# Edge stage of a graph attention kernel: eight block numbers with one register load on TensorE and on VectorE

## The reference

```
qi = q[dst]
kj = k[src]
vj = v[src]
alpha = jnp.sum(qi * kj, axis=-1) / jnp.sqrt(jnp.float32(D))
m = jax.ops.segment_max(alpha, dst, num_segments=n)
ex = jnp.exp(alpha - m[dst])
denom = jax.ops.segment_sum(ex, dst, num_segments=n)
a = ex / (denom[dst] + 1e-16)
out = jax.ops.segment_sum(a[..., None] * vj, dst, num_segments=n)
```

## Time and profile before

| what | value |
|---|---|
| median of three runs | 1348.41 us |
| span of the profiled execution, first to last instruction | 1474.8 us |
| edge stage in it, first to last `prod` | 95.1 to 815.0 us |
| busy in the span: PE, DVE, POOL, ACT | 84%, 72%, 63%, 54% |
| DVE busy from 200 to 750 us | 426.0 of 550 us |
| TensorE clock granted from 200 to 750 us | 0.89 |
| block numbers loaded by PE, by DVE | 232, 261 |

### The profile page before, as it was taken

How to read it: one execution, slowest core, us unless ns; L and a number is a source line. 1 busy time by engine, 2 the same in 40 slices (tenths; PEclk the granted TensorE clock), 3 DMA queues, 4 the chain that set the end, 5 groups by cost and what they waited for, 6 DMA issues and landing times. The chain is left out here.

```text
span 1474.8 us, 24100 instructions
## 1 busy us (share of the span) xinstructions
PE 1233.3 (84%) x6835; PEld 952.7 (65%) x6835; DVE 1068.6 (72%) x2557; ACT 802.2 (54%) x2505; POOL 924.8 (63%) x885
## 2 busy tenths in 40 slices
PE   7988676766776777767676889999999999999998
PEld 3444454544444544545454478889798899999998
DVE  7646887777877777877788779886757655556655
ACT  1265857575847575666657555555543344444443
POOL 3366566666666665666664556866766477667765
PEclk9999989899888898888989999999999999999999
DMA  7477766676766666767675120101000000000002
GB/s 229 157 225 211 235 192 193 183 203 184 200 187 196 188 200 179 202 185 204 181 199 145 38 70 29 52 28 42 8 15 22 1 22 15 10 21 15 1 12 77
DMA packets 74087, 175.39 MB, mean 119 GB/s; under 512 B 11516, under 2 KB 36667, under 8 KB 73961
## 3 DMA queue, kind: packets, MB, share of 16 engines
q0 software_dynamic: 37632, 124.28, 30.3%
q1 hardware_dynamic: 34657, 48.25, 9.9%
q10 hardware_dynamic: 1672, 1.33, 0.3%
HBM read 159.91 MB, written 13.91 MB: 118 GB/s over the span
## 5 line engine op out<-in xcount | busy, mean ns | idle before, releaser
L694 POOL DMA_INDIRECT ring<-kv_rows,k_srcI x464 | 465.1, 1002 | 280.8 <-issue 121.5
L764 ACT ACTIVATE ring<-ring 128x64 f32<-128x64 f32 x1800 | 439.8, 337 | 15.0 <-issue 13.4
L1297 POOL TENSOR_TENSOR wm<-k_gf,wm 128x512 fp32r<-128x512 f32 (+2 forms) x224 | 259.6, 1163 | 143.4 <-DVE wm L1798 143.4
L1396 ACT ACTIVATE k_gf<-psF,k_scT 128x512 f32<-128x512 f32 (+2 forms) x224 | 162.3, 725 | 251.9 <-PE psF L1567 237.6
L814 PE MATMUL psA<-ring,oh 128*128 128x260 f32 x912 | 273.4, 428 | 6.6 <-DVE k_acc L1023 5.4
L784 PE MATMUL psQ<-k_q,ohT 128*128 x1392 | 221.1, 300 | 66.7 <-issue 63.3
L1798 DVE CAST wm<-k_gf 128x512 fp32r<-128x512 f32 (+2 forms) x224 | 160.2, 722 | 155.3 <-ACT k_gf L1396 155.3
L989 DVE TENSOR_TENSOR prod<-psQ,ring 128x512 f32<-128x512 f32 x232 | 157.5, 679 | 82.2 <-remote 28.3
L784 PEld LDWEIGHTS psQ<-k_q,ohT 128*128 128x128 bf16 x1392 | 128.8, 103 | 123.0 <-issue 93.9
L814 PEld LDWEIGHTS psA<-ring,oh 128*128 128x128 f32 x912 | 177.3, 216 | 33.8 <-ACT ring L764 6.3
L1029 DVE TENSOR_REDUCE alpha<-prod 128x8 f32<-128x512 f32 x232 | 155.7, 671 | 0.2
(11 more groups left out here) (283 smaller groups left out, 2644.9 us busy)
## 6 DMA issues: line engine op xcount, KB each, us to landing
ohT<-step_destinations SPq DMA_DIRECT2D x29, 512.0 KB
ring<-kv_rows,k_srcI POOLq DMA_INDIRECT x464
kv_rows<-kvst SPq DMA_DIRECT2D x25, 260.0 KB, 2.6
we<-in_L_ffn_W SPq DMA_DIRECT2D x16, 256.0 KB, 2.8
residual<-qst SPq DMA_DIRECT2D x25, 128.0 KB
xs<-in_x SPq DMA_DIRECT2D x2, 1024.0 KB, 9.1
resin<-residual SPq DMA_DIRECT2D x4, 512.0 KB, 4.5
we<-in_L_ffn_Wo SPq DMA_DIRECT2D x8, 256.0 KB, 2.8
```

Of the source, the lines that this page charges most:

```text
L694: nc.gpsimd.indirect_dma_start(out=ring[:, LT * (j % CP) + k, j // CP:j // CP + 2, :].rearrange("p t e -> p (t e)"), out_offset=None, in_= ...
L764: last = nc.scalar.activation(row[:, 0:D], row[:, 0:D], ACT.Copy, scale=row[:, D:HW_])
L1297: nc.gpsimd.tensor_tensor(low[:, i % 2, m, 0:w], gf[:, n % 4, 0:w], high[:, i % 2, m, 0:w], ALU.subtract).then_inc(s_gl, 1)
L1396: nc.scalar.activation(gf[:, n % 4, 0:cols(g)], ps, ACT.Relu, bias=bias, scale=scale).then_inc(s_ev, 1)
```

## The change

Both engines load eight block numbers at once, into eight registers, with one TENSOR_LOAD a chunk, and without the check of the bounds. PE does so in `expand` where `jj` is 0. DVE does so where it rescales; the registers then serve the rescaling and the eight additions that follow, and the load at the head of every `at` is gone. The values, the matmuls and the vector operations stay as they are.

```
+        def blocks(engine, first):
+
+            n = min(CP, STEPS - first)
+            _, got = nc.values_load_multi_w_load_instructions(
+                brow[0:1, first:first + n], engines=[engine], min_val=0, max_val=NB - 1,
+                skip_runtime_bounds_check_because="a step's block is a count of block borders, made on the chip between 0 and NB - 1")
+            return got
+
...
+            held = {}
+
             def expand(i, j, fresh):
...
-                blk = nc.tensor.value_load(brow[0:1, bass.ds(step, 1)], min_val=0, max_val=NB - 1)
+                if jj == 0:
+                    held[0] = blocks(mybir.EngineType.PE, step)
+                blk = held[0][jj]
...
                 if live(i, j, fresh, ADD_LAG):
                     b = step - ADD_LAG
-                    blk = nc.vector.value_load(brow[0:1, bass.ds(b, 1)], min_val=0, max_val=NB - 1)
+                    blk = held[0][b % CP]
...
-                    blk = nc.vector.value_load(brow[0:1, bass.ds(br, 1)], min_val=0, max_val=NB - 1)
+                    held[0] = blocks(mybir.EngineType.DVE, br)
+                    blk = held[0][0]
                     dve.wait_ge(s_mv, NV * m + V_FAC)
```

## The result

| | before | changed |
|---|---|---|
| median | 1349.61 us (17 runs, 1346.42 to 1351.88) | 1354.01 us (17 runs, 1346.56 to 1362.29) |
| span of the profiled execution | 1474.8 us (the one of the earlier trace rows) | 1344.9 us |

The ratio is 1.0036, with a 95% interval from 1.0022 to 1.0049: slower by 4.4 us where 7.3 us were forecast. Measured again later (experiment 10), the same kernel had 1.0006, from 0.9993 to 1.0018. The two intervals don't overlap: a small loss the first time, none the second. The medians give no gain in either.

What follows compares the result with a forecast made beforehand. The prediction took DVE's chain of vector instructions to bound the edge stage. Its terms, -3.5 + 14.8 - 4 = +7.3 us on the median of 1348.4 us, gave 1355.7 us, range 1336 to 1384 us.

Steps and rivals of the forecast that it cites:

- What bounds the kernel: Edge stage: DVE's chain of vector instructions bounds it in the runs, about 2.5 us a step, with PE ahead.
- The surplus of the profiled span: Edge stage: the profiled span's 126 us over the median run is idle time mostly not in the runs.
- Removed, 1: DVE's load and check in 232 steps, covered by queued vector work: 0 in seven steps of eight.
- Removed, 2: DVE's second load, in the step after the rescaling, goes: 0.12 us exposed a chunk, -3.5 us.
- Changed, 3: DVE's load of eight before the rescaling: 1.38 us with 0.87 us free, delaying the rescaling each chunk, +14.8 us.
- L: The length of one load of eight numbers, taken as 1.38 us, bounded between 0.31 and 2.46 us.
- the first rival: DVE's wide load is cheap, up to 0.87 us, so the rescaling isn't delayed: -7.5 us, 1341 us, chance 33%.
- the rival with 17%: The load of eight: 0.2 us for each further number, slower than before; chance 17%.
- Removed, 4: PE's load and check go in 203 steps, counting only where DVE waits for PE: -4 us.
- Changed, 5: PE's load of eight delays a chunk's first group by 0.9 us, covered by 1.5 us: 0.
- Nothing changes: The queue's deeper cover in the runs hides both the exposed 0.12 us and the rescaling's delay: 1348 us, chance 12%.
- my own sign of being wrong in substance: If L is small and nothing is gained, the runs have no exposed sequencer time at all.

Runs made afterwards that it cites:

- experiment 10: The changed kernel unaltered, measured again beside the kernel before: 1349.56 us, ratio 1.0006.
- 6: The kernel before, but from the 33rd step on SyncE copies the second tile of a step instead of its being gathered: 1333.23 us.
- 7: The changed kernel, but from the 33rd step on SyncE copies the second tile of a step instead of its being gathered: 1323.38 us.
- c0: The kernel before, unchanged, profiled a second time: 1349.05 us (one run), span 1347.4 us.
- experiment 1: The kernel before with PE's half of the change alone; VectorE keeps one load and check a step: 1347.98 us, ratio 0.9991.
- 2: The kernel before with VectorE's half of the change alone; PE keeps its load and check a step: 1352.69 us, ratio 1.0024.
- 3: The kernel before with one load a step kept on both engines, only the bounds check removed: 1351.19 us, ratio 1.0017.
- 12: The changed kernel with the comparison that makes `ohT` cut from 2048 columns to one from the fifth chunk on: 1338.89 us, ratio 0.9937 against experiment 10.

## Why the prediction was right or wrong

The sign and the range were right by luck, the reason was not. The forecast's +14.8 us is a cost that doesn't exist and its -7.5 us a gain that can't show; with the right length of the load the same reasoning would have said 1341 us.

- *What bounds the kernel.* Wrong. I said that VectorE's chain bounds the edge stage in the runs. It does in 6 and 7. In the kernels themselves VectorE first waits over 0.3 us for a gather at 335 us in c0 and at 271 us in the changed kernel; until then the gathers are ahead, though they run at their own pace from 148 us on. From there POOL's gathers hold the pace, 20.0 us a chunk and more. The step that failed is the first: I read 353 of 550 us of POOL as slack. Its busy time leaves out the 0.30 us between two gathers, and the profile's row for it had 121.5 us of "issue". 8 x 2 x 1.25 = 20.0 beside 19.5 us was there to be worked out.
- *The surplus of the profiled span.* That it isn't in the runs was right. That it comes with the profiler was no sound thought: c0 is profiled and has none, and 18 plain runs had it. Of the 39 waits ahead of the product that I laid to PE's results, lays 14 to PE.
- *Removed, 1.* 0 for seven steps, right: intervals of 2.18, 2.15, 2.61, 2.25 us and so on are the same in both.
- *Removed, 2*, -3.5 us: the pause did go, 2.47 to 2.34 us; its worth to the kernel was 0, since the gathers hold the pace. With half of the gathers it paid.
- *Changed, 3*, +14.8 us: mis-sized. L is 0.598 us, not 1.38; the spare time is 1.05, not 0.87. The term is 0. The mechanism exists, with L = 1.60 us, and even then cost 2.5 us and not 16. The measured L agrees with the first rival, "a wide load is cheap"; its time, 1341 us, failed by the same wrong bound. The 0.153 us that I took for each further number was an estimate, half a lone load. The 0.2 us a further number of the rival with 17%, which stands in the chances, no run shows: a further number took 0.042 us with 8 and (1.602 - 0.306) / 23 = 0.056 us with 24. That the load starts when the queue takes no more holds as far as this: in c0 26 of the 29 loads at L1040 start within 0.004 us of the start of the mask L1007, three vector instructions ahead of the rescaling. That a lone load's 0.306 us is a wait for an answer and not work, no run shows.
- *Removed, 4*, -4 us: 0, by experiment 1.
- *Changed, 5*: 0, right.
- *The rivals and the signs.* "Nothing changes", 1348 us, came nearest in time, but not for its reason: the exposed 0.12 us was there and went. L is small and nothing was gained, which was my own sign of being wrong in substance; what I would have concluded from it, that no sequencer time is exposed, is wrong too. PE's "issue" waits fell to a fifth, not an eighth, and a third of all its waiting there was left.
- *What is left.* The sum of true terms is 0, the measured difference 4.4 us once and 0.6 us once. Experiments 2 (+0.24%) and 3 (+0.17%) point to VectorE's half, with the reserve on the tail given there, and 10, the whole change, has no loss. A gather that begins while VectorE runs a mask or the comparison is longer, by 0.20 and 0.46 us on average, and the removed pause moves every such instruction by 0.12 us against POOL; that this is the cause was argued, not shown. Each of the two measurements has its median outside the other's interval, so something that differs between them matters as much as the change. It may be the chip; neither kernel was run twice on one known chip to tell.

No version here beats both kernels with the right output where the kernel before takes 1349 us. The largest handle that the runs show is not in the changed lines: the gathers' pace (6 and 7) and the comparison that lengthens them (12).

## What to carry to other kernels

Work out the period of every engine that issues work, from start to start and not from its busy time, before naming the bound: in c0 POOL was busy 306.8 of 400 us (77%) and held the pace. Time taken from an engine that then waits for another came back here as that wait (27.1 us on average with the pause, 33.1 without), and the row "who waited for it" shows it; but compare several profiles, since this row alone differed by 4 us between two kernels with the same code on VectorE. Profile the kernel before a second time when its span and its runs disagree.

## What the runs showed of the hardware

- A load of registers from SBUF took 0.306 us for one number, 0.598 for 8, 1.602 for 24: 0.04 to 0.06 us for each further one.
- An indirect gather of 128 rows took 0.946 us, and the next one started 0.305 us after its end, never later than 0.32 us while nothing held it; those pauses don't count as busy (307 gathers in 400 us of c0: 306.8 us busy). It took some 1.48 us (median) when it met the bf16 comparison of 2048 columns (by the five profiles of c0, 1 to 3 and the change, 124 gathers during which it was the last vector instruction running 0.1 us after their start took 0.46 us more on average). Without most of the comparison (12) the gathers of the stage's second half took 5.5 us in all beyond 0.946 us each, with it (10) 16.1. Why the comparison lengthens a gather, no run shows.
- The same holds for the masks (two SBUF operands): 209 gathers with one running 0.1 us after their start took 0.20 us more on average, 92% of them over 1.0 us. A mask that started 0.2 to 0.3 us after the gather went with 1.42 to 1.50 us (the 6 long gathers of 12). Of 542 gathers met by a product, with one operand in PSUM, 5% took over 1.0 us.
- One and the same kernel took 1349 or 1467 us, the latter on one chip of three. There VectorE stands idle for 1 to 4 us about twice a chunk, ahead of products, but also ahead of instructions that wait for PE alone and whose matmuls had ended by the trace. In the first profile PE's last `psA` ended at 572.52 us, VectorE was free at 572.77, and the addition that reads it started at 574.32. With half of the gathers (6 and 7, same chip) that is gone, and the kernel takes 1333 us. Why is open; the traces of that chip have no landing times of the gathers, so late gathers aren't excluded for the products.
